# Softmax inverse sums: spread to the rows of their heads by two DMAs through DRAM instead of TensorE transposes and ScalarE copies

## The reference

```python
q = (x @ Wq).reshape(b, lq, H, DK).transpose(0, 2, 1, 3)
kv = (y @ Wkv).reshape(b, lkv, 2, H, DK).transpose(2, 0, 3, 1, 4)
k, v = (kv[0], kv[1])
atten = jax.nn.softmax(jnp.einsum('bhid,bhjd->bhij', q, k) * SCALE, axis=-1)
res = jnp.einsum('bhij,bhjd->bhid', atten, v)
res = res.transpose(0, 2, 1, 3).reshape(b, lq, H * DK)
out = res @ Wproj + bproj
...
x = x + _L0_xattn_ref(_layernorm(x, axis=-1), ctx_768, ...)
x = x + _L0_ffn_ref(_layernorm(x, axis=-1), ...)      # top 2 of 8 experts
```

## Time and profile before

| | |
|---|---|
| median of 3 runs | 1570.44 us |
| the profiled execution | 1568.5 us, span 1566.4 us |
| PE busy | 1503.0 us, 96% |
| DVE, ACT, POOL busy | 62%, 49%, 35% |
| attention part | about 25 to 1195 us |
| expert part | about 1225 us to the end |
| one pair of batches | 72.6 us |

### The profile page before, as it was taken

The page is one execution under the profiler, slowest core; times in us unless marked ns, Lnnn a source line. Parts: engine busy times, 40 slices in busy tenths (PEclk is TensorE's granted clock), DMA queues, the critical chain, the costliest instruction groups (busy, mean ns, idle before and its releaser), DMA issues. The chain is left out here.

```text
span 1566.4 us, 37570 instructions
## 1 busy us (share of the span) xinstructions
PE 1503.0 (96%) x12134; PEld 1321.0 (84%) x12135; DVE 968.7 (62%) x2579; ACT 762.3 (49%) x2091; POOL 555.2 (35%) x636
## 2 busy tenths in 40 slices
PE   4999999999999999999999999999996699999997
PEld 4888888898888888888888888898875588888886
DVE  5667677676766676767767676667675633333332
ACT  3555555555555555555555555555553322222221
POOL 5224233333433243423334343324355122323232
PEclk9999999999999999999999999999997799999999
DMA  5411111111112221111111111221016233332332
GB/s 152 131 50 50 56 49 55 49 55 50 54 54 60 64 73 54 49 54 49 54 49 57 49 54 54 65 69 52 12 66 227 52 52 51 50 54 47 53 50 28
DMA packets 82704, 96.19 MB, mean 61 GB/s; under 512 B 6912, under 2 KB 77808, under 8 KB 82672
## 3 DMA queue, kind: packets, MB, share of 16 engines
q1 hardware_dynamic: 68960, 74.67, 16.5%
q0 software_dynamic: 12144, 15.66, 6.2%
q10 hardware_dynamic: 1568, 5.44, 1.0%
HBM read 44.85 MB, written 50.90 MB: 61 GB/s over the span
## 5 line engine op out<-in xcount | busy, mean ns | idle before, releaser
L767 ACT ACTIVATE prob<-bank,neg_max 112x375 f32<-112x375 f32 x512 | 295.3, 586 | 138.1 <-DVE neg_max L1017 138.1
L1017 DVE TENSOR_REDUCE neg_max<-bank 112x1 f32<-112x375 f32 x512 | 243.9, 539 | 19.4 <-PE bank L1247 19.3
L1257 PE MATMUL bank<-ident,prob 112*125 112x112 f32 x1536 | 214.7, 274 | 2.6 <-ACT prob L767 2.4
L1257 PEld LDWEIGHTS bank<-ident,prob 112*125 112x125 f32 x1536 | 195.9, 188 | 13.8 <-ACT prob L767 4.9
L706 POOL DMA_INDIRECT out<-y_out,dest_now x63 | 97.8, 1552 | 244.1 <-ACT y_out L859 215.0
L895 DVE TENSOR_TENSOR K_l<-bank,K_h 128x376 fp32r<-128x376 f32 x256 | 140.4, 550 | 64.9 <-ACT K_h L727 62.4
L1281 PE MATMUL bank<-probT,V 125*64 125x112 f32 x3072 | 176.6, 264 | 2.0 <-DVE probT L1023 1.1
L1155 PE MATMUL bank<-Wgu,hT_h 128*128 x504 | 175.1, 429 | 2.9 <-DVE hT_l L1112 2.9
L1281 PEld LDWEIGHTS bank<-probT,V 125*64 125x64 f32 x3072 | 149.1, 137 | 14.6 <-issue 2.6
L885 DVE COPY V<-bank 125x512 f32<-125x512 f32 x96 | 66.4, 692 | 151.3 <-PE bank L1219 147.4
L1133 DVE COPY hidT<-bank 128x512 f32<-128x512 f32 x63 | 43.6, 692 | 173.7 <-PE bank L1462 173.7
(11 more groups left out here) (171 smaller groups left out, 3719.9 us busy)
## 6 DMA issues: line engine op xcount, KB each, us to landing
bins<-pad_rows SPq DMA_DIRECT2D x29, 1032.0 KB, 6.2
h_in<-bins SPq DMA_DIRECT2D x63, 129.0 KB, 2.2
y_sb<-in_ctx SPq DMA_DIRECT2D x32, 187.5 KB, 2.4
y_sb<-in_ctx SPq DMA_DIRECT2D x62, 93.8 KB, 2.5
Wgu<-in_L_ffn_gate_up_w SPq DMA_DIRECT2D x4, 1024.0 KB, 5.2
Wgu<-in_L_ffn_gate_up_w ACTq DMA_DIRECT2D x4, 1024.0 KB, 13.2
x_sb<-in_x SPq DMA_DIRECT2D x16, 224.0 KB, 2.8
x_res<-in_x SPq DMA_DIRECT2D x32, 112.0 KB, 5.6
```

The lines of the kernel that those rows point to most:

```text
L767: nc.scalar.activation(prob[:, j, :], S_ps[j][0:LQ, 0:LKV], ACT.Exp, bias=neg_max[:, j:j + 1], accum_out=row_sum[:, head // HB, head % HB: ...
L1017: nc.vector.tensor_reduce(neg_max[:, j:j + 1], S_ps[j][0:LQ, 0:LKV], AX.X, ALU.max, negate=True).then_inc(max_done, 1)
L1257: last = nc.tensor.transpose(S_ps[j][0:KR, t * LQ:t * LQ + LQ], prob[:, j, t * KR:t * KR + KR], ident[0:LQ, 0:LQ])
```

## The change

All but the last of the 64 halves go another way. DVE writes the eight reciprocals into a 128 x 32 block (reordered, even heads first) and transposes it in blocks of 32 x 32 (`inv_sumT`). SP then writes that to a DRAM tensor `sums` (128 rows of 128 bytes), waits until it has landed, and reads it back into `inv_rows`, each of two rows of 2 KB to 64 partitions. DVE's `normalise` waits for the second DMA (`rows_in`). The last half keeps the transposes of PE and the copy of ACT. `inv_rows` has a buffer for each half, `prefill` moves ahead in SP's order, and `normalise` of `half` 1 moves behind the copies of turned weights and the low part of Q in step 0.

```diff
+            def spread_inverses(b, half):
+                n = 2 * b + half
+                sp.wait_ge(inv_done, n + 1)
+                sp.sem_inc(passed, 1)
+                if not known(b) or b >= 1:
+                    sp.wait_ge(rows_in[half], 16 * b)
+                sp.dma_start(sums[half].rearrange("h (i r) -> i h r", r=32), inv_sumT[:, half, :]).then_inc(sums_out[half], 16)
+                sp.wait_ge(sums_out[half], 16 * b + 16)
+                sp.sem_inc(passed, 1)
+                if not known(b) or b >= 1:
+                    sp.wait_ge(O_done, n - 1)
+                sp.dma_start(inv_rows[:, half].rearrange("p c q -> p (c q)"),
+                             sums[half, 0:HB, :].rearrange("(r c) q -> r (c q)", r=2).unsqueeze(1)
+                             .to_broadcast([2, DK, HALF * P])).then_inc(rows_in[half], 16)
...
+                    if there(b + 2, STRIDE // P):
+                        sp.wait_ge(prefilled[odd], 16 * (i + 1))
+                        prefill(b + 2, odd)
+                    if there(b, B):
+                        spread_inverses(b, 0)
                     if known(i) and i == NP - 1 and odd:
                         sp.wait_ge(made, a.made(a.find(0, "q", 7)))
                         load_expert(sp, 1)
...
+                    if there(b, B) and not (known(b) and b == B - 1):
+                        spread_inverses(b, 1)
                     if not known(i) or i + 2 < NP:
                         sp.wait_ge(y_lo, b + 3)
...
-                        if s % 2 and there(b, B):
-                            copy_inverses(2 * b + s // 2)
+                        if known(b) and b == B - 1 and s == 3:
+                            copy_last_inverses()
...
+                nc.vector.reciprocal(inv_sum[0:LQ, half, 0:HB].rearrange("p (r c) -> p c r", r=2),
+                                     row_sum[:, half, :].rearrange("p (c r) -> p c r", r=2)).then_inc(inv_small, 1)
                 dve.wait_ge(inv_small, n + 1)
...
+                nc.vector.transpose(inv_sumT[:, half, :], inv_sum[:, half, :]).then_inc(inv_done, 1)
+            def normalise(b, half):
+                n = 2 * b + half
+                if known(b) and b == B - 1 and half:
+                    dve.wait_ge(inv_out, 1)
+                else:
+                    dve.wait_ge(rows_in[half], 16 * b + 16)
                 dve.wait_ge(pv_made, 2 * n + 2)
...
-                        if s == 0 and there(b - 1, B):
-                            normalise(2 * b - 1)
                         if s == 2 and there(b, B):
-                            normalise(2 * b)
+                            normalise(b, 0)
...
                         for k in made_at["early"] + made_at["mid"]:
                             low_part(a, k)
+                        if s == 0 and there(b - 1, B):
+                            normalise(b - 1, 1)
...
-                        if s == 1 and there(b, B):
-                            ...
-                            turn_inverses(2 * b)
...
-                        if s == 3 and there(b, B):
-                            ...
-                            turn_inverses(2 * b + 1)
+                        if known(b) and b == B - 1 and s == 3:
+                            pe.wait_ge(hnT_done, b)
+                            turn_last_inverses()
```

More of the change, by code:

```diff
@@ L194, in attention_and_experts @@
     tokens = out[0:TOK, :].rearrange("(b q) c -> b q c", q=LQ)
+    sums = nc.dram_tensor("sums", [2, 32, P], F32).ap()
     bins = nc.dram_tensor("bins", [E * STRIDE + IDLE * P, W], F32).ap()
@@ L363, in attention_and_experts @@
         inv_done, O_done = sem("inv_done"), sem("O_done")
-        inv_small, inv_turned, inv_out = sem("inv_small"), sem("inv_turned"), sem("inv_out")
+        inv_small, inv_wide_done, inv_turned, inv_out = (sem(n) for n in ("inv_small", "inv_wide_done", "inv_turned", "inv_out"))
+        sums_out, rows_in = [[sem(f"{n}{half}") for half in range(2)] for n in ("sums_out", "rows_in")]
         OT_hi, OT_lo = sem("OT_hi"), sem("OT_lo")
@@ L773, in turned, with copy_last_inverses @@
                 nc.scalar.copy(probT[:, j, :], S_ps[j][0:KR, 0:KT * LQ]).then_inc(probT_second, 1)
[L775 to L780, removed]
+            def copy_last_inverses():
+                act.wait_ge(inv_turned, 1)
+                act.wait_ge(O_done, 2 * B - 2)
+                nc.scalar.copy(inv_rows[:, 1, :, 0:LQ], C_ps[:, 0:HALF * LQ].rearrange("p (c q) -> p c q", c=HALF)).then_inc(inv_out, 1)
             def pair(i):
@@ L929, in _, with invert_sums @@
             split_context(1, 1)
-            def invert_sums(n, half):
+            def invert_sums(b, half):
+                n = 2 * b + half
                 dve.wait_ge(exp_done, HB * n + HB)
-                if not known(n) or n >= 1:
-                    dve.wait_ge(inv_turned, n)
-                nc.vector.reciprocal(inv_sum[:], row_sum[:, half, :]).then_inc(inv_small, 1)
+                if known(b) and b == 0:
+                    dve.wait_ge(consts, N_CONSTS)
+                nc.vector.reciprocal(inv_sum[0:LQ, half, 0:HB].rearrange("p (r c) -> p c r", r=2),
+                                     row_sum[:, half, :].rearrange("p (c r) -> p c r", r=2)).then_inc(inv_small, 1)
@@ L937, in invert_sums @@
                 dve.wait_ge(inv_small, n + 1)
[L938 to L943, removed]
+                if known(b) and b == B - 1 and half:
+                    nc.vector.tensor_copy(inv_wide[:].rearrange("p (c r d) -> p c r d", c=HALF, r=2),
+                                          inv_sum[0:LQ, 1, 0:HB].rearrange("p (r c) -> p c r", r=2).unsqueeze(3)
+                                          .to_broadcast([LQ, HALF, 2, DK])).then_inc(inv_wide_done, 1)
+                    return
@@ L944, in normalise @@
+                if not known(b) or b >= 1:
+                    dve.wait_ge(sums_out[half], 16 * b)
+                nc.vector.transpose(inv_sumT[:, half, :], inv_sum[:, half, :]).then_inc(inv_done, 1)
+            def normalise(b, half):
+                n = 2 * b + half
+                if known(b) and b == B - 1 and half:
+                    dve.wait_ge(inv_out, 1)
+                else:
+                    dve.wait_ge(rows_in[half], 16 * b + 16)
                 dve.wait_ge(pv_made, 2 * n + 2)
-                if not known(n) or n >= 1:
+                if not known(b) or n >= 1:
@@ L946, in normalise @@
                     dve.wait_ge(OT_lo, n)
-                nc.vector.tensor_tensor(O_now[:], O_ps[:, 0:HALF * LQ], inv_rows[:], ALU.mult).then_inc(O_done, 1)
+                nc.vector.tensor_tensor(O_now[:].rearrange("p (c q) -> p c q", c=HALF),
+                                        O_ps[:, 0:HALF * LQ].rearrange("p (c q) -> p c q", c=HALF),
+                                        inv_rows[:, half, :, 0:LQ], ALU.mult).then_inc(O_done, 1)
             def residual(i, b, slot):
@@ L1284, in weigh, with turn_last_inverses @@
                 last.then_inc(pv_made, 1)
-            def turn_inverses(n):
-                pe.wait_ge(inv_done, n + 1)
+            def turn_last_inverses():
+                pe.wait_ge(inv_wide_done, 1)
                 for j in range(HALF):
@@ L1350, in pair @@
                             if s == 0:
[L1351 to L1354, removed]
+                                free_bank(a, k)
                             elif there(b - 2, B):
@@ L1360, in pair @@
                         if s == 2 and there(b - 1, B):
-                            if there(b, B):
-                                pe.wait_ge(inv_out, 2 * b + 1)
+                            n = a.at(odd, 1, "early") if a else []
+                            if n:
+                                pe.wait_ge(lo_done, a.split(n[0]))
                             else:
```

27 lines of the change are left out of this document (9 added, 18 removed).

## The result

The changed kernel takes 1714.22 us (median of 4 runs, 1709.44 to 1722.33) and the one before 1570.71 us in the same series: 1.092 times as long, 95% interval 1.090 to 1.095. I had predicted 1634 us and a range of 1538 to 1705 us. The direction was right, the size was not.

The account below looks back on a forecast made before the run. PE, busy for 96% of the span, was taken to bound the kernel. 1568.5 us + 56 (loop, removed work already counted) + 7.5 (end) = 1632 us, and 1.9 us from profile to median: 1634 us, range 1538 to 1705 us.

Parts of the forecast that it names:

- removed sets: PE's sets of four transposes ahead of `weigh`, gone from 31 and 30 halves: 30.8 us less.
- the stalls of the loop: PE waiting ahead of `weigh`: net +0.77 us by `half` 1, +1.07 us by `half` 0, +56 us in all.
- What bounds the kernel: Attention part: PE almost never idle, so each microsecond of PE work removed or wait added moves the result equally.
- What is removed: Transposes ahead of `weigh` in steps 1 and 3: PE gains 0.5 us by half, 30.8 us in all.
- The budget for L: How long L may be before PE waits: 8.5 us for `half` 1, 8.25 us in the mean for `half` 0.
- L: Time from `inv_done` on DVE to `inv_rows` ready for DVE, two DMAs and hand-overs: 9.8 us.
- Two and four engines: The first new DMA runs on four engines, 2.3 us, the second on two, 7.0 us; L 9.8 us.
- the estimate of L near 5.1 us: Other rule for the two DMAs, 2.0 us plus bytes over 436 GB/s: 2.0 and 2.6 us, everything hidden.
- SP's later issues at nothing: Context, `x_sb`, `x_res` and `prefill` issued some 3 us later in a batch, behind the second DMA: no cost.
- The clock: PE's granted clock in the loop mostly holds, so the same work costs 0 us more.
- the rival: PE's clock falls often in the loop; chance 0.07.
- The end of the attention part: Last batch: expert 1's load goes out later, POOL and the last projection wait: +7.5 us, +0.6 us if hidden.

Follow-up runs that it names:

- Experiment 6: experiment 2 with `prefill` moved back behind the context loads: 1538.84 us, ratio 0.981 to the kernel before.
- experiment 7: experiment 2 with the inverses spread for the first batch only, all later halves using batch 0's rows: 1541.76 us, ratio 0.982 to the kernel before.
- Experiment 4: Changed kernel, with SP issuing nothing behind the second DMA of `half` 1 until it has landed: 1668.05 us, ratio 1.064 to the kernel before.
- kernel with two reads: Changed kernel, with the second DMA cut into two reads, each with 64 rows outermost: 1553.49 us, ratio 0.989 to the kernel before.
- experiment 2: The kernel with two reads, with the loads of experts 1 and 2 issued ahead of the last batch's spread: 1546.55 us, ratio 0.985 to the kernel before.
- experiment 8: Changed kernel, slow second DMA kept, `prefill` back behind the context loads and expert loads ahead of the last spread: 1718.77 us, ratio 1.094 to the kernel before.
- experiment 5: Changed kernel, with the second DMA cut in two by columns, each half still with two blocks outermost: 1830.53 us, ratio 1.166 to the kernel before.

## Why the prediction was wrong, step by step

Experiment 6 has the same PE instructions as the changed kernel and no waits in the loop, so PE's busy time can be compared directly: 1532.3 against 1477.5 us, 54.8 us more for the same work. With that the 146.0 us of the span part into three. That the third is the clock, the traces bear out: from 100 to 1300 us the granted clock is 0.96 in the mean in the changed kernel and 1.00 from 100 to 1160 us in experiment 6, and 0.04 of 1200 us is 48 us.

| term | predicted | measured |
|---|---|---|
| removed sets | -30.8 us | -25.5 us (1503.0 to 1477.5 busy) |
| PE idle | +94.3 us | +116.7 us |
| same work at a lower clock | 0 | +54.8 us |
| sum | +63.5 us | +146.0 us |

The predicted idle time is 56 + 30.8 us for the stalls of the loop and 7.5 us for the end.

- **What bounds the kernel**: right. Each microsecond of PE's waits came out in the end.
- **What is removed**: 0.41 us by half, not 0.5 (experiment 7). I took the distance from the first transpose to the first product of `weigh`, but the hand-over from the V product to whatever follows it is 0.09 us longer with `weigh`. I had named that as a rival and let it be all or nothing.
- **The budget for L**: right to about 0.1 us. With L of 10.6 and 9.7 us, budgets of 8.5 and 8.25 us give waits of 2.1 and 1.45 us; PE shows 2.2 and, without the first batch, 1.2 us, and 0.1 us by batch at L1344.
- **Two and four engines**: right. 2 and 4 small packets, 87 ns by row of 2 KB where I took 86, 2.1 us from the first issue to the second where I had 2.3 + 0.25 us, and some 7.4 us for the second copy of `half` 0 (916.87 to 924.38 less the hand-over) where I had 7.0 us. The rule of the Trainium skill's "DMA: Bandwidth & Descriptors", section "Why a DMA increments its semaphore by 16 and not by 1", agrees with these packets; the estimate of L near 5.1 us by the same page's "Anatomy of one DMA" does not agree with the measured 9.7 us. That section gives its figures for DMAs that GpSimd issues, which the prediction did not say; these are issued by SP.
- **SP's later issues at nothing**: wrong. I asked whether they would come too late, and not what they would do to a copy still under way: they go out while the second DMA of `half` 1 runs on its two engines, and slow it. It takes 8.6 us instead of 7.4 us (896.06 to 904.75, less the hand-over), and L is 10.6 us and not 9.8 us. Experiment 4 takes 1 us of this back. It is 30 x 0.9 = 27 us of idle time; `half` 0 waited somewhat less than I had, and 22 us were missing in all. It also brought about half of what the clock cost: experiment 4 takes back 27.8 of the 54.8 us.
- **The clock**: this is the step that failed, with the largest share. I read slices of full clock (digit 9) over a loop without gaps and held it to stay ("mostly to hold", a chance of 0.07 for the other case) although no row showed PE with such gaps. It did fall, for 54.8 us. The 4 us at 1.2 GHz by gap, 2 us more, that I gave the rival came from no row, and turned out near: between 100 and 1300 us the trace has 27 stretches at the lower clock, 99 us in all, with 49 us of work lost in them, 1.8 us each. No row could tell how often it would happen. The rival belonged in the sum, or at least in the range: 1634 us and half of 122 us is 1695 us.
- **The end of the attention part**: the chain was as I described it, POOL waiting for expert 1:

```profile
1314.05 0.98 SPq L402 DMA_DIRECT2D Wgu<-in_L_ffn_gate_up_w  x2
...
1325.41 1.89 POOL L634 CAST Wgu<-Wgu 128x2048 fp32r<-128x2048 f32 x1 [17.31 <-DMA Wgu<-in_L_ffn_gate_up_w]
1327.38 4.52 POOL L628 TENSOR_TENSOR Wgu<-Wgu 128x2048 fp32r<-128x2048 f32 x1
1331.88 0.25 POOL L697 TENSOR_SCALAR std<-mv 112x1 f32<-112x1 f32 x1
```

  The load landed 11.4 us after its issue (I had 9.0 us). In the kernel with two reads the order costs 6.9 us, and for that case the prediction had only 0.6 us. There the load took 6.5 us (1158.02 to 1164.56 us; I had 4.8). And POOL could have come to the normalisation of batch 30 sooner than I took: with the loads ahead (experiment 2) it does so 7.5 us behind the first DMA of the spread (1155.58 to 1163.10 us), where the prediction had it some 11 us behind, as in the kernel before. So the chain was right and its price for fast reads was not. In the changed kernel the price could not be told from the rest (experiment 8).
- **The start** was not in the sum: the first batch's spread stands behind a third `prefill`. In the kernel with two reads that is 5.4 to 7.7 us (experiments 2 and 6).

How steeply the time goes with L shows best in four kernels with the same PE instructions:

| kernel | L, `half` 1 and 0 | PE busy | span |
|---|---|---|---|
| experiment 6 | no wait in the loop | 1477.5 us | 1536.5 us |
| experiment 4 | 9.6 and 9.9 us | 1504.5 us | 1663.2 us |
| changed | 10.6 and 9.7 us | 1532.3 us | 1712.4 us |
| experiment 5 | 11.4 and 11.0 us | 1584.5 us | 1829.0 us |

From the changed kernel to experiment 5 the mean L grows by 1.05 us. I had 61 us for each microsecond; the span grew by 117 us, 52 of them PE's longer busy time.

What stays open: which gaps bring the clock down. In the changed kernel each of the 27 stretches begins beside a gap of PE. It was so for 24 of the 26 gaps of 1.9 us and more, all in step 0, and for 3 of the 30 gaps between 0.9 and 1.5 us, most of them in step 2. So the gaps that the prediction had in mind (1.3 to 1.6 us) seldom brought the clock down here; those of step 0, longer than forecast since SP's issues stood behind the second DMA, nearly always did. Length alone is no rule either: in experiment 5, 26 of 45 gaps between 0.9 and 1.5 us had such a stretch beside them.

## To carry to other kernels

Before a small DMA goes on a tight path, look at its outermost dimension on both sides and not at its bytes: two blocks of 64 rows ran on 2 engines and made a kernel 9% slower, the same rows as two reads of 64 made it faster. Ask also what is issued right behind it: here that cost the small DMA 1 us. And where a change gives a busy TensorE its first gaps, price the clock too until a row shows that it holds: here each microsecond of added idle time came with 0.3 to 0.6 us of longer busy time (experiments 4 and 5 and the changed kernel, each against experiment 6).

## What the runs showed of the hardware

- A copy with 2 blocks outermost ran on 2 engines, one with 4 on 4 and one with 64 on 16 (2, 4 and 16 small packets beside the data); 256 KB took 7.4 us on two and two reads of 128 KB 2.9 us each. Two such copies, issued one behind the other, took 8.6 us together (experiment 5, from issue at 909.51 us to `normalise` at 918.09 us), as on the same two engines; on two pairs of engines an estimate from the rows was 5.0 us. The trace does not name the engines.
- Loads issued behind a copy on two engines slow it and are slowed: L of `half` 1 was 10.6 us with them and 9.6 us without, and the loads of 93.8 KB landed in 6.8 us and in 2.6 us (experiment 4).
- Behind gaps of 1.33 and 2.41 us the granted clock was 0.50, and 24 products took 2.51 us instead of 1.37 us. Products that nobody used, put in the gaps, kept it at 1.00 and saved 30 us of 1714 us.
